# Edge values of a graph-attention layer: edge targets loaded as a row and spread over the partitions by a product of ones

## What is computed

```
src, dst = edge_index[0], edge_index[1]
q = (x @ Wq + bq).reshape(n, H, C)         # H = 8 heads, C = 32
k = (x @ Wk + bk).reshape(n, H, C)
v = (x @ Wv + bv).reshape(n, H, C)
e = (edge_attr @ We).reshape(-1, H, C)
kj = k[src] + e
alpha = jnp.einsum('ehc,ehc->eh', q[dst], kj) / jnp.sqrt(jnp.float32(C))
...
msg = (v[src] + e) * alpha[:, :, None]
out = jax.ops.segment_sum(msg, dst, num_segments=n)
```

## Time and profile before

| | |
|---|---|
| median of three runs | 6938.87 us (6933.76 to 6942.06) |
| the profiled execution, its own time | 7003.0 us |
| its span, first to last instruction | 7001.2 us |
| mean granted TensorE clock | 0.814 of full speed |
| busy: TensorE, DVE, ScalarE, GpSimd | 4860.9, 3942.7, 2369.7, 2991.1 us |
| moved by DMA | 819.11 MB, mean 117 GB/s |
| `edge_values` in the span | about 5468 to 6129 us |

### The profile page before, as it was taken

The page is one execution under the profiler, slowest core; times in us unless marked ns, Lnnn a source line. Parts: engine busy times, 40 slices in busy tenths (PEclk is TensorE's granted clock), DMA queues, the critical chain, the costliest instruction groups (busy, mean ns, idle before and its releaser), DMA issues. The chain is left out here.

```text
span 7001.2 us, 80027 instructions
## 1 busy us (share of the span) xinstructions
PE 4860.9 (69%) x19231; PEld 3375.8 (48%) x19232; DVE 3942.7 (56%) x8585; ACT 2369.7 (34%) x5719; POOL 2991.1 (43%) x2932
## 2 busy tenths in 40 slices
PE   2677749637775947775577756888799555467999
PEld 2444526425444734443344433444587433356777
DVE  3555643446667246666366665666424788787333
ACT  1333412123333223433344324555321122265333
POOL 2555432445552045553555526666100577643000
PEclk8777859868887968887788868899899766687999
DMA  4454414234442024443444422121001799954000
GB/s 117 139 159 155 118 42 137 89 96 142 138 147 66 14 91 141 137 146 92 126 145 137 144 50 35 30 31 30 18 13 42 270 376 369 324 189 142 10 14 23
DMA packets 543459, 819.11 MB, mean 117 GB/s; under 512 B 87966, under 2 KB 421967, under 8 KB 542839
## 3 DMA queue, kind: packets, MB, share of 16 engines
q0 software_dynamic: 140832, 376.78, 19.2%
q1 hardware_dynamic: 396388, 432.93, 19.1%
q10 hardware_dynamic: 5907, 5.92, 0.3%
HBM read 658.06 MB, written 157.71 MB: 117 GB/s over the span
## 5 line engine op out<-in xcount | busy, mean ns | idle before, releaser
L783 POOL DMA_INDIRECT l_edges_stage<-l_h_rows,src_t x832 | 802.7, 965 | 687.0 <-issue 223.7
L1096 PE MATMUL l_edges_ps_sum<-l_edges_msg,l_edges_hot 128*128 128x264 f32 x1664 | 602.7, 505 | 262.3 <-DVE l_attn_acc L925 182.3
L2510 POOL DMA_INDIRECT l_edge_kv<-l_kv_rows,src_t x416 | 479.1, 1152 | 668.3 <-POOLq L2417 517.7
L2938 POOL DMA_INDIRECT l_gate_edges_srow<-l_gate_src_rows,l_gate_edges_idx x512 | 487.1, 951 | 330.9 <-issue 141.7
L3074 PE MATMUL l_gate_edges_ps<-l_gate_edges_wide,l_gate_edges_hot_lo 128*128 128x500 f32 x1024 | 507.9, 639 | 103.8 <-issue 77.0
L1096 PEld LDWEIGHTS l_edges_ps_sum<-l_edges_msg,l_edges_hot 128*128 128x128 f32 x1664 | 360.0, 241 | 423.4 <-DVE l_attn_acc L925 258.8
L2563 PE MATMUL l_edge_ps_q<-l_q_q,l_edge_hot 128*128 x832 | 338.0, 577 | 324.9 <-issue 193.5
L783 POOL DMA_INDIRECT l2a_edges_stage<-l2a_h_rows,src_t x416 | 401.9, 966 | 338.4 <-issue 114.4
L783 POOL DMA_INDIRECT l2b_edges_stage<-l2b_h_rows,src_t x416 | 401.7, 966 | 331.7 <-issue 115.5
L2563 PEld LDWEIGHTS l_edge_ps_q<-l_q_q,l_edge_hot 128*128 128x128 f32 x832 | 230.1, 289 | 432.7 <-issue 387.2
L1096 PE MATMUL l2a_edges_ps_sum<-l2a_edges_msg,l2a_edges_hot 128*128 128x272 f32 x832 | 304.5, 510 | 159.3 <-DVE l2a_sums_acc L925 101.1
(11 more groups left out here) (784 smaller groups left out, 10845.6 us busy)
## 6 DMA issues: line engine op xcount, KB each, us to landing
l_edge_e<-e_rows SPq DMA_DIRECT2D x416, 128.0 KB
l_val_rows<-l_edge_vj SPq DMA_DIRECT2D x104, 512.0 KB
l_agg_stage<-l_val_rows SPq DMA_DIRECT2D x52, 1024.0 KB, 5.5
l_edges_rel_b<-rel_rows SPq DMA_DIRECT2D x52, 512.0 KB
l_edges_ea<-in_edge_attr SPq DMA_DIRECT2D x48, 512.0 KB
e_rows<-l_edges_e_s SPq DMA_DIRECT2D x48, 512.0 KB
l_experts_w<-in_L_ffn_w SPq DMA_DIRECT2D x32, 512.0 KB, 5.1
l_gate_edges_lo_b<-l_gate_edges_lo_rows SPq DMA_DIRECT2D x64, 256.0 KB
```

Of the source, the lines that this page charges most:

```text
L783: nc.gpsimd.indirect_dma_start(out=stage[:, c % SL, u, :], out_offset=None, in_=h_rows, in_offset=bass.IndirectOffsetOnAxis(ap=K.src_t[:, ...
L1096: nc.tensor.matmul(ps_sum[u][:], hot[:, g, u, :], msg[:, g % 2, u, :], start=True, stop=True).then_inc(summed, 1)
L2510: nc.gpsimd.indirect_dma_start(out=kv[:, m, u, :], out_offset=None, in_=kv_rows, in_offset=bass.IndirectOffsetOnAxis(ap=K.src_t[:, n * EB ...
L2938: nc.gpsimd.indirect_dma_start(out=srow[:, n % 4, u, :], out_offset=None, in_=src_rows, in_offset=bass.IndirectOffsetOnAxis(ap=idx[:, n * ...
```

## The change

In `edge_values` the targets of four batches (2048 bf16 numbers, 4 KB) are loaded as one row onto partition 0, into one of three places of `rel`; SP issues that load with every fourth batch. A tile `one` of 128 ones on one partition is set by DVE at the start. TensorE multiplies `one` with 512 columns of the row, a product with a contraction of one, which leaves the row on all 128 partitions of a PSUM bank (`ps_rel`, two of them). ScalarE reads its first pass from there. TensorE's order becomes: targets of batches 0 and 1, then for each batch its products and the targets of the batch two further on. A targets product waits for its row (`rel_in`) and for ScalarE's first pass of the batch that used the bank before (`hot_near`); ScalarE now waits for `spread` where it waited for the transfer.

```diff
--- before.py
+++ after.py
@@ -2483,20 +2483,24 @@
     ES = 2
     UB = 4
     NBE = STEPS // EB
+    RB, RS = 4, 3
+    PB = 2
     with Phase(nc, name) as ph:
         kv = ph.sb("kv", [P, UB, EB, 2 * D])
         e = ph.sb("e", [P, UB, EB, D])
-        rel_b = ph.sb("rel_b", [P, UB, EB * P], BF16)
+        rel = ph.sb("rel", [1, RS, RB * EB * P], BF16)
+        one = ph.sb("one", [1, P], BF16)
         nrow = ph.sb("nrow", [P, 1])
         hot = ph.sb("hot", [P, ES, EB * P])
         vj = ph.sb("vj", [P, ES, EB, D])
         red = ph.sb("red", [P, ES, EB, HEADS])
+        ps_rel = [ph.psum(f"ps_rel{m}", [P, EB * P]) for m in range(PB)]
         ps_q = [ph.psum(f"ps_q{m}", [P, 2, D]) for m in range(2 * ES)]
-        nrow_made, hot_near, hot_built, q_made, kj_made, v_made, prod_made, red_made, lg_made = (
-            ph.sem(s) for s in ("nrow_made", "hot_near", "hot_built", "q_made", "kj_made", "v_made", "prod_made", "red_made", "lg_made"))
+        nrow_made, hot_near, hot_built, q_made, kj_made, v_made, prod_made, red_made, lg_made, one_set, spread = (
+            ph.sem(s) for s in ("nrow_made", "hot_near", "hot_built", "q_made", "kj_made", "v_made", "prod_made", "red_made", "lg_made", "one_set", "spread"))
         kv_in = [ph.sem(f"kv_in{m}") for m in range(UB)]
         e_in = [ph.sem(f"e_in{m}") for m in range(UB)]
-        rel_in = [ph.sem(f"rel_in{m}") for m in range(UB)]
+        rel_in = [ph.sem(f"rel_in{m}") for m in range(RS)]
         stored = [ph.sem(f"stored{m}") for m in range(ES)]
 
         with nc.Block() as block:
@@ -2521,9 +2525,11 @@
                         sp.wait_ge(v_made, n - UB + 1)
                     for u, first in enumerate(firsts):
                         sp.dma_start(e[:, m, u, :], K.e_rows[bass.ds(first, P), :]).then_inc(e_in[m], 16)
-                    if n >= UB:
-                        sp.wait_ge(hot_near, n - UB + 1)
-                    sp.dma_start(rel_b[:, m, :], over_partitions(K.rel_rows[n * EB:(n + 1) * EB, :].rearrange("s e -> (s e)"))).then_inc(rel_in[m], 16)
+                    if n % RB == 0:
+                        r = n // RB
+                        if r >= RS:
+                            sp.wait_ge(spread, (r - RS + 1) * RB)
+                        sp.dma_start(rel[0:1, r % RS, :], K.rel_rows[n * EB:(n + RB) * EB, :].rearrange("s e -> (s e)").unsqueeze(0)).then_inc(rel_in[r % RS], 16)
 
                 def store(n):
                     sp.wait_ge(v_made, n + 1)
@@ -2543,15 +2549,26 @@
                 act.wait_ge(nrow_made, 1)
                 for n in range(NBE):
                     s = n % ES
-                    act.wait_ge(rel_in[n % UB], 16 * (n // UB + 1))
+                    act.wait_ge(spread, n + 1)
                     if n >= ES:
                         act.wait_ge(q_made, n - ES + 1)
-                    nc.scalar.activation(hot[:, s, :], rel_b[:, n % UB, :], ACT.Abs, bias=nrow[:]).then_inc(hot_near, 1)
+                    nc.scalar.activation(hot[:, s, :], ps_rel[n % PB][:], ACT.Abs, bias=nrow[:]).then_inc(hot_near, 1)
                     act.wait_ge(hot_near, n + 1)
                     nc.scalar.activation(hot[:, s, :], hot[:, s, :], ACT.Relu, bias=K.ones[:, 0:1], scale=-1.0).then_inc(hot_built, 1)
 
             @block.tensor
             def _(pe):
+                def targets(n):
+                    r = n // RB
+                    pe.wait_ge(rel_in[r % RS], 16 * (r // RS + 1))
+                    if n >= PB:
+                        pe.wait_ge(hot_near, n - PB + 1)
+                    at = n % RB * EB * P
+                    nc.tensor.matmul(ps_rel[n % PB][:], one[:], rel[0:1, r % RS, at:at + EB * P], start=True, stop=True).then_inc(spread, 1)
+
+                pe.wait_ge(one_set, 1)
+                targets(0)
+                targets(1)
                 for n in range(NBE):
                     s = n % ES
                     if n % 4 == 0:
@@ -2563,6 +2580,8 @@
                         last = nc.tensor.matmul(ps_q[2 * s + u // 2][:, u % 2, :], hot[:, s, u * P:(u + 1) * P],
                                                 q[:, bass.ds(ids[n % 4 * EB + u], 1), :].rearrange("p a d -> p (a d)"), start=True, stop=True)
                     last.then_inc(q_made, 1)
+                    if n + PB < NBE:
+                        targets(n + PB)
 
             @block.vector
             def _(dve):
@@ -2572,6 +2591,7 @@
                                                    ALU.mult, ALU.add).then_inc(lg_made, 1)
 
                 nc.vector.tensor_scalar(nrow[:], K.row[:], -1.0, None, ALU.mult).then_inc(nrow_made, 1)
+                nc.vector.memset(one[:], 1.0).then_inc(one_set, 1)
                 masks.make(dve)
                 for n in range(NBE):
                     m, s = n % UB, n % ES
```

## The result

The changed kernel takes **6954.47 us** (median of 20 runs, 6946.08 to 6970.92) against 6939.2 us for the kernel before (20 runs): ratio 1.0023, interval 1.0016 to 1.003, so 15 us slower where 33 us faster was forecast. I therefore compare the stage itself, from the start of the first gather to the end of the last reduction: 660.5 us before (5467.8 to 6128.3), 667.1 us after (5429.2 to 6096.2). What follows the stage takes 872.9 and 872.5 us.

The account below looks back on a forecast made before the run. The prediction took transfers to bound edge_values, with TensorE, ScalarE and DVE following. Its terms, -35.1 + 0.3 + 0.2 + 1.5 (late product), gave -33 us, from 6938.9 to 6906 us, range 6880 to 6937.

Parts of the forecast that it names:

- the price of the bytes: Removed target loads in edge_values, 13.63 MB of queue traffic at 388 GB/s: 35.1 us saved.
- 2.23 MB / 388 GB/s = 5.76 us: Bytes of one edge_values batch at full rate, taken to explain the steady pitch of 5.71 us.
- GpSimd takes over the pace: Rival: gathers in edge_values keep the 5.7 us pitch, only 22.7 us of buffer waits can go, 6916; chance 0.22.
- The rule of 435 GB/s: Rule against the change: the fabric ceiling leaves the stage 12% to spare, so removing 6% of bytes brings 0 us.
- my row: Profile row of a quiet stretch at 388 GB/s, DMA share 1.06, taken as full rate against the 435 GB/s ceiling.
- slower: the product behind the row: Rival: TensorE's wait for the row in targets(4r) delays product 4r-1; 30 us slower, 6969; chance 0.10.
- The stalls go as well: Rival: fewer bytes also clear half the slow stretches of edge_values, another 24 us, 57 in all, 6882; chance 0.13.
- held up by the queue itself: SP's issues of e, four in 4.11 us, wait on the queue, so 78 fewer transfers to issue save nothing.
- The small terms: Row loads 0.3 us, memset 0.2; spreading product 0.64 us per batch hidden on TensorE; ScalarE's PSUM read nothing.

Follow-up runs that it names:

- four variants with the bytes gone: Changed kernel with three kv buffers, four target tiles, product unused, or product twice; ratios to the kernel before 0.9968, 0.9966, 0.9961, 0.9962.
- set 3: Those four variants on the chip where the kernel before takes 6170 us; the 90.8 us is from every product of ones made twice, ratio 0.9962.
- the three lengths above: Longest batch on chips with stalls: changed kernel with three gather buffers 12.3 us, with four 14.9 to 16.2, with five 19.7.

## Why the prediction was wrong

**The step that failed** is the price of the bytes: "At the full rate of 388 GB/s they cost 13.63 / 0.388 = 35.1 us ... zero if the queues are not the bound. I take 35.1 us, because L2583's idle time says that the queue's delay reaches DVE." L2583's idle time did say so, and removing the bytes removed it in the quiet batches (61 to 6 us). What I did not ask was who waits next. The same rows gave the answer: 479.1 us of gathers and 127.9 us of gaps are 607 of 661 us in which GpSimd had no slack. The stage could lose only GpSimd's 22.7 us of waits, what its gathers lose beside DVE, and part of the 31.8 us of tail. In place of -35.1 us the bytes alone measured -5 and +4 us (6998.80 against 7003.76, 6943.97 against 6939.86; both not told from zero) with stalls. On the chip without stalls four variants with the bytes gone save 19 to 27 us of 6170; each differs from the changed kernel in something else, and the kernel before was not traced there, so how much of that is the bytes stays open.

**2.23 MB / 388 GB/s = 5.76 us** was right for a quiet batch and wrong for the stage. The median batch is 5.74 or 5.75 us in all five traces with the bytes on chips with stalls, and 5.45 or 5.46 with the bytes gone alone, while GpSimd's instructions are the same: in quiet stretches the bytes do set the pitch. But four gathers at 1.15 us and four gaps of 0.305 are 5.83 us, nearly the same number (my rival had 5.7), and that one holds for the average. The likely reading is that batches come faster only while gathers made during a stall are still in the buffers; over the stage DVE gets no more batches than GpSimd gathers. The experiments without e and with three gathers part the two: without e the median batch is 4.98 us and the stage still 643 us. The Trainium skill ("Perfetto Trace Analysis", What "DMA-bound" means) names the second case: the queue of the issuing engine is solid with issues, and that time goes into making descriptors, not into moving data. The trace agrees as far as the share goes, 479 + 128 of 661 us on GpSimd; what that time goes into it doesn't show.

**The rival "GpSimd takes over the pace"** named the right engine and put 0.22 on it. Its pitch was wrong (the median fell to 5.33 us), its ceiling of 22.7 us was passed by no run with all gathers on a chip with stalls (without e the whole kernel gained 12.5 us), and its last clause, "if the stalls stay too, nothing", is nearest to what happened. It did not see that waits could grow. Of the gathers of the changed kernel, the 62 that take over 1.6 us (the stage's first one left out) overlap L2600 and L2603 by 0.84 and 0.83 us in the mean, the 314 short ones by 0.10 and 0.04; beyond 0.95 us each the 416 gathers lose 78 us in all, nearly what they lost before (84). The Trainium skill ("SBUF — State Buffer", Who interferes with whom) states the exclusion; the trace agrees.

**The rule of 435 GB/s** (the Trainium skill, "DMA: Bandwidth & Descriptors", Specifications) would have given 0 us, and on chips with stalls nothing told from 0 came. The runs don't bear out its reason: the best 40 us of every trace but the one without e lie between 385 and 392 GB/s, with four gathers or three, with the bytes or without, so my row looks like a bound of the quiet stretches. What brought the 0 was GpSimd's pace.

**The rival "slower: the product behind the row"** had the right sign by the wrong mechanism. DVE's waits for the product, 81 us, would lie at every fourth batch, 4r-1; by the batch number modulo four they are 21, 32, 10 and 18 us, of which the last is the place in question. In set 3 TensorE waited 90.8 us for the row and DVE not at all.

**"The stalls go as well"** was the opposite of what happened. With stalls on the chip, they did not come from the queue falling behind in bytes: a quarter of the bytes fewer leaves 22 of them, a quarter of the gathers fewer leaves 3. That SP's issues are "held up by the queue itself", as the prediction has it, is in doubt too: its register instructions, which issue nothing, are slow as well, and without e TensorE's signals are late while SP issues nothing at all.

**The small terms** stand: the product of ones took 0.49 us (0.64 taken) and by itself costs nothing that can be told (ratios 1.0 and 1.0007 with the bytes kept); ScalarE's first pass out of PSUM took 0.686 us against 0.722.

**Open:** what starts a stall; why TensorE's signals and SP's instructions are late in it; why fewer bytes mean more waiting for GpSimd. That a stall ends when the gathers pause fits the three lengths above and the absence of stalls where GpSimd has slack, but only in part the signals: of the ten waits of over 4 us before L2608 in the changed kernel's trace, seven ended 0.7 to 3.1 us after the last gather before a pause, and three while the gathers ran on. Why one chip has none isn't known either. No version that does all of the work was faster than the kernel before, beyond its interval, on a chip with stalls.

## What to carry to other kernels

Before pricing bytes by the queue's rate, add up the busy time and the fixed gaps of each engine over the whole stage, the one that issues the gathers first: an engine whose sum, with what follows its last instruction (here 607 + 31 of 661 us), comes within a few per cent of the stage is the first suspect for the bound, even when a faster steady pitch is to be seen. A pitch that two resources explain equally well needs a look for which of them has idle time in the stage. And a gain in the quiet stretches counts only if it reaches the engine that sets the sum; otherwise the buffers fill and it comes back as waits.

## What the runs showed of the hardware

- The chips differ far more than the change: the kernel before takes 6170 us on one and 6939 to 7008 us on the others, and variants of this edit are worth -0.3 to -0.4% there, the edit itself +0.1 to +0.2% on the others.
- In the stalls SP's issues of e come 2 to 3.5 us apart (four in 2.5 us in quiet stretches of the changed kernel) and TensorE's signals come up to 19 us after the modelled end of the product (24 with five buffers), while DVE's are prompt (GpSimd starts 0.27 us after the reduction it waits for, at 5514.39) and GpSimd's gathers run at their fastest, 0.95 us.
- SP's register instructions slow down with them. Steps of over 0.6 us, of 832: 148 to 219 in all traces on chips with stalls that have the four gathers and the loads of e, 21 with three gathers, none in the four on the chip without stalls. Ends of stalls and ends of such steps fall together (5511.55).
- Over 40 us, 385 to 392 GB/s was the most in every trace but the one without e (305).
- The product of ones reads 512 bf16 columns on one partition in 0.39 us at the full clock and 0.60 us at the low one.
